# Second layer of a fused four-layer kernel: later lower parts, and four routed blocks made ahead

## The reference

```python
gates = sigmoid(x @ w_gate)                       # per token, head and expert
gm = one_hot(argmax(gates)) * gates
values = einsum('bhne,ehdk,bnd->bhnk', gm, value_experts, x)
attn = softmax(causal(q * SCALE @ k.T))
out = einsum('bhij,bhjk->bhik', attn, values)
out = einsum('bhne,ehkd,bhnk->bhnd', gm, output_experts, out).sum(axis=1)
```

## Time and profile before

| | us |
|---|---|
| median of 3 runs | 3399.88 (3398.44 to 3403.79) |
| the profiled execution | 3397.21 |
| its span | 3395.2 |
| TensorE busy in it | 3192.8 |
| granted clock, mean | 0.974 |

### The profile page before, as it was taken

The page is one execution under the profiler, slowest core; times in us unless marked ns, Lnnn a source line. Parts: engine busy times, 40 slices in busy tenths (PEclk is TensorE's granted clock), DMA queues, the critical chain, the costliest instruction groups (busy, mean ns, idle before and its releaser), DMA issues. The chain is left out here.

```text
span 3395.2 us, 49636 instructions
## 1 busy us (share of the span) xinstructions
PE 3192.8 (94%) x18098; PEld 2292.6 (68%) x18098; DVE 1852.0 (55%) x3126; ACT 1479.7 (44%) x2732; POOL 959.2 (28%) x883
## 2 busy tenths in 40 slices
PE   7998999999999999999999898999989899999998
PEld 4667656975588755986569545555455588888886
DVE  4557745675466743866455665756657423333332
ACT  3331254423543144422543575555746544444443
POOL 1213323742266512753237301103020011111110
PEclk9998999999999999999999899999999899999999
DMA  6112111011111111111111101010000210000000
GB/s 199 65 41 67 32 31 55 26 50 38 26 55 50 40 27 33 56 44 35 28 55 38 27 2 51 2 27 1 2 26 2 95 57 13 13 13 13 7 7 13
DMA packets 182672, 124.06 MB, mean 37 GB/s; under 512 B 125216, under 2 KB 163360, under 8 KB 178976
## 3 DMA queue, kind: packets, MB, share of 16 engines
q1 hardware_dynamic: 182432, 120.87, 12.7%
HBM read 103.37 MB, written 28.44 MB: 39 GB/s over the span
## 5 line engine op out<-in xcount | busy, mean ns | idle before, releaser
L1667 ACT ACTIVATE l3b_prob<-sums 128x512 f32<-128x512 f32 (+3 forms) x768 | 333.0, 494 | 169.1 <-PE sums L1578 130.9
L1939 PE MATMUL sums<-l_uhi,l_h 128*128 128x512 f32 x1024 | 405.6, 396 | 0.0
L1939 PE MATMUL sums<-l_ulo,l_h 128*128 128x512 f32 x1024 | 405.1, 396 | 0.0
L644 POOL TENSOR_TENSOR l_qrow<-l_vm,l_qst 128x512 fp32r<-128x512 f32 x256 | 352.5, 1389 | 162.0 <-ACT l_qst L638 134.5
L1027 DVE TENSOR_REDUCE l2b_mx<-sums 128x1 fp32r<-128x1024 f32 (+7 forms) x256 | 192.6, 758 | 267.2 <-PE sums L939 265.5
L964 PE MATMUL sums<-sb_nx,l_vx 128*128 128x512 f32 (+3 forms) x768 | 306.2, 509 | 2.2 <-ACT l_od L1002 2.2
L995 ACT ACTIVATE sb_nx<-sums 128x512 f32<-128x512 f32 (+3 forms) x384 | 183.4, 493 | 260.7 <-PE sums L956 255.5
L2024 DVE TENSOR_TENSOR l_ulo<-l_made,l_uhi 128x512 fp32r<-128x512 f32 x128 | 90.3, 705 | 363.4 <-ACT l_uhi L1956 363.3
L1573 PE MATMUL sums<-l_qst,l_kst 64*128 64x512 f32 (+3 forms) x768 | 276.5, 422 | 11.9 <-ACT l3b_prob L1667 5.4
L631 DVE TENSOR_TENSOR l_vm<-l_oT,sums 128x512 f32<-128x512 f32 x256 | 174.3, 683 | 166.0 <-PE sums L623 164.3
L638 ACT CAST l_qst<-l_vm 128x512 fp32r<-128x512 f32 x256 | 157.9, 620 | 243.9 <-DVE l_vm L631 231.8
(11 more groups left out here) (272 smaller groups left out, 8005.0 us busy)
## 6 DMA issues: line engine op xcount, KB each, us to landing
l_ve<-ve SPq DMA_DIRECT2D x32, 512.0 KB, 4.1
l_oe<-oe SPq DMA_DIRECT2D x16, 1024.0 KB, 5.2
between<-sb_x SPq DMA_DIRECT2D x48, 256.0 KB, 2.1
l_vm<-weights_copy SPq DMA_DIRECT2D x32, 352.0 KB, 3.4
sb_nx<-between SPq DMA_DIRECT2D x9, 1024.0 KB, 5.7
weights_copy<-h SPq DMA_DIRECT2D x2, 4096.0 KB, 26.1
l_ve<-inverse SPq DMA_DIRECT2D x32, 256.0 KB, 3.6
l_qst<-l3b_peak SPq DMA_DIRECT2D x512, 0.5 KB, 2.0
```

The lines of the kernel that those rows point to most:

```text
L644: pool.tensor_tensor(rlo[:, i % RT, :], routed[:, i % RT, :], rhi[:, i % RT, :].bitcast(F32), ALU.subtract).then_inc(s3.routed_lo, 1)
L1667: act.activation(prob[:, i % RB, j, a, 0:hi - lo], bank(m.ps, part % SCORE, 0, hi - lo), ACT.Exp, scale=SCALE1).then_inc(s.exp_ready, 1)
L1939: run(lambda out, a, x, first, last: pe.matmul(out, a, x, start=first, stop=last))
```

## The change

`lo_parts` of a projection's fourth piece moves on VectorE from tick 23 (39, 55) to tick 24 (40, 56), behind that tick's reduction. Four blocks instead of three are made ahead; their masks begin at tick 75 instead of 78, routes at 76 instead of 79, upper parts at 77 instead of 80. Block 3's mask reuses bank 4 and waits for the first route, block 4's takes bank 7 and block 5's bank 6; so the last check of the weights, which must be through with its buffer, is taken at tick 75 instead of 78. The copy of the last head's output moves from the end of ScalarE's list in attention to the start of its list in the output stage, with a semaphore `last_od` for which SP's transfer of head 7's denominators and the mask of block 5 wait. Each sequence does this.

```diff
--- before.py
+++ after.py
@@ -482,7 +482,7 @@
            "gates_hi hilo_ready gates_turned gmT_ready")
 ATTN2 = ("qk_mm qk_hi qk_parts max_mm max_read row_ready even_carried odd_carried score_mm exp_ready pv_mm o_read "
          "den_in den_turned row_in rden_in o_ready oe_in even_weight_in odd_weight_in weight_chain weight_unlike weight_taken")
-OUT2 = ("ve_in oe_in1 oe_in2 oe_in3 oe_hi oe_lo "
+OUT2 = ("last_od ve_in oe_in1 oe_in2 oe_in3 oe_hi oe_lo "
         "mask_mm routed routed_hi routed_lo out_mm y_ready last_den_in last_den_turned last_row_in last_rden_in last_o_ready")
 CLAMP = 80.0
 
@@ -528,8 +528,8 @@
     gates_hi = od[:, 1, 0:N].bitcast(F32R)
     hilo = od[:, 0, :].rearrange("p (t a n) -> p t a n", t=NT, a=2)
     blocks = [(c, e, n) for c in range(H0 // 2) for e in range(NE) for n in range(NH)]
-    MASKS, AHEAD = 3, 3
-    mask_bank = lambda i: (4, 7, 3)[i] if i < AHEAD else 4 + i % MASKS
+    MASKS, AHEAD = 3, 4
+    mask_bank = lambda i: (4, 7, 3, 4, 7)[i] if i <= AHEAD else 4 + i % MASKS
     EH = NE // 2
     half = lambda odd: slice(DH0 * odd, DH0 * odd + DH0)
     vcol = lambda h: half(h % 2)
@@ -866,8 +866,9 @@
         DIVIDED = H0 - 2
         divided_in = lambda x: divmod(x - 3 * NT, NT)
         ROW_OUT, TURNED, ROW_BACK, SPREAD, CHUNK_AT = 3, 5, 5, 7, 1
+        LAST_CHECK = 75
         SPLIT_HI, SPLIT_LO = {60: 0, 62: 1}, {73: 0, 74: 1}
-        MASK_AT, ROUTE_AT, ROUTE_HI_AT = {78: 0, 79: 1, 80: 2}, {79: 0, 80: 1, 81: 2}, {80: 0, 81: 1, 82: 2}
+        MASK_AT, ROUTE_AT, ROUTE_HI_AT = ({at + i: i for i in range(AHEAD)} for at in (75, 76, 77))
 
         def project_in(x):
             c, ahead = divmod(x - PROJECT_FROM, 2 * NT)
@@ -981,6 +982,8 @@
                         weighted(h2, k2)
                     if x in MASK_AT:
                         pe.wait_ge(s.max_read, NT * H0)
+                        if MASK_AT[x] >= MASKS:
+                            pe.wait_ge(s3.routed, MASK_AT[x] - MASKS + 1)
                         mask(pe, MASK_AT[x])
 
             @block.scalar
@@ -1015,7 +1018,6 @@
                         act.copy(ohi0[:, es, :], oe[:, es, :]).then_inc(s3.oe_hi, 1)
                     if x in ROUTE_HI_AT:
                         route_hi(act, ROUTE_HI_AT[x])
-                head_out(H0 - 1)
 
             @block.vector
             def _(dve):
@@ -1025,10 +1027,12 @@
                         t = NT - 1 - k1
                         dve.wait_ge(s.max_mm, NT * h1 + k1 + 1)
                         dve.reduce_max(mx[:, h1, t:t + 1], bank(m.ps, max_bank(h1, k1), 0, (t + 1) * P), AX_X).then_inc(s.max_read, 1)
-                    if project_in(x):
+                    if project_in(x) and project_in(x)[1] < 3:
                         lo_parts(dve, *project_in(x))
-                    if k1 == NT - 2 and h1 >= 1:
-                        dve.wait_ge(s.weight_unlike, h1)
+                    if project_in(x - 1) and project_in(x - 1)[1] == 3:
+                        lo_parts(dve, *project_in(x - 1))
+                    if (k1 == NT - 2 and 1 <= h1 < H0) or x == LAST_CHECK:
+                        dve.wait_ge(s.weight_unlike, min(h1, CHECKS))
                         dve.scalar_tensor_tensor(worst[:, :], unlike, 0.0, worst[:, :], ALU.not_equal, ALU.max).then_inc(s.weight_taken, 1)
                     over, k = divided_in(x)
                     if 0 <= over < DIVIDED and k == TURNED:
@@ -1088,7 +1092,7 @@
         stats_at = {4: 0, 5: 1, 6: 2, 7: 3}
         LAST_TURNED, last_o_at = 4, {23: (6, 0), 26: (6, 1), 29: (7, 0), 32: (7, 1)}
         VALUE_HI_AT, value_lo_at = 51, {53: 0, 55: 1}
-        PER_C = NE * NH
+        PER_C, PV = NE * NH, 5
         following = b + 1 < SEQS
         if not following:
             turn_at, x_hi_at, x_lo_at, value_lo_at, LOGITS_AT, GATES_FROM, EXP_AT, VALUE_HI_AT = {}, {}, {}, {}, None, len(blocks), None, None
@@ -1101,6 +1105,8 @@
             @block.sync
             def _(sp):
                 for h in (6, 7):
+                    if h == H0 - 1:
+                        sp.wait_ge(s.last_od, 1)
                     sp.dma_start(denp[:, h % 2, :], den_row(h)).then_inc(s.last_den_in, 16)
                 fetch_load(sp, m, sf, src[b + 1])
                 sp.wait_ge(s.oe_lo, 2)
@@ -1139,6 +1145,7 @@
                         act.wait_ge(s.out_mm, PER_C * (c - 1))
                     act.copy(ohi_of(c, es), oe[:, es, :]).then_inc(s.oe_hi, 1)
 
+                act.copy(od[:, (H0 - 1) % 2, :], m.ps[:, PV * HALF:(PV + 2) * HALF]).then_inc(s.last_od, 1)
                 for i in range(AHEAD, len(blocks)):
                     if i in split_at:
                         expert_hi(*split_at[i])
@@ -1214,6 +1221,8 @@
                 for i in range(AHEAD, len(blocks) + AHEAD):
                     if i < len(blocks):
                         pe.wait_ge(s.routed, i - MASKS + 1)
+                        if i == AHEAD + 1:
+                            pe.wait_ge(s.last_od, 1)
                         mask(pe, i)
                     k = i - AHEAD
                     c, e, n = blocks[k]
```

## The result

The changed kernel takes 3351.5 us (median of four runs, 3349.9 to 3355.8) against 3400.0 for the kernel before (four runs, 3398.4 to 3403.8): 48.5 us less. The ratio is 0.9858, with a 95% interval of 0.9846 to 0.987. Measured again beside later experiments, the same kernel had 0.9874 (0.9859 to 0.9889), 43.5 us less. The forecast was 3354, or 46 less.

What follows compares the result with a forecast made beforehand. TensorE, busy 94% of the span, was taken as the bound, with time only in idle gaps and half clock. Terms 17.0 + 15.0 + 6.0 + 6.5 + 1.5 = 46.0 us gave a 3354 us median, own bounds 3342 to 3366, rivals 3338 to 3372.

Steps and rivals of the forecast that it cites:

- The late reduction: Where heads 2, 4 and 6 begin: reducing before the lower parts wins 1.42 us 12 times, 17.0 us.
- The second gap: At the next row of maxima after each projection: TensorE waits 0.37 to 0.43 us for the delayed 896-column reduction.
- The clock: Behind the 12 projection gaps: ten half-clock stretches of TensorE go, 1.5 us each, 15.0 us.
- The border: Between attention and output experts: barrier opens 1.96 us earlier, token load 0.5 later, 1.5 us four times, 6.0 us.
- Slack in the output stage: Masks issued four blocks ahead remove waits of 0.57 and 1.60 us: 6.5 us, plus 1.5 us of halved clock.
- my slower rival: In the output stage TensorE stands before block k until route k+1; at 0.3 us per block, 3425 us; chance 0.03.

Runs made afterwards that it cites:

- The filled gaps: Kernel before with nine unused 512-column matmuls in each of the twelve 2.23 us gaps: 3378.9 us, ratio 0.9938.
- the tokens first: Changed kernel with the load of the next tokens issued ahead of both denominator transfers in the output stage: 3350.8 us, ratio 0.986.
- the lower parts alone: Kernel before with only a projection's fourth lower parts one tick later, still three blocks ahead: 3364.5 us, ratio 0.9902.
- four ahead alone: Changed kernel with a projection's fourth lower parts put back to their old tick: 3389.4 us, ratio 0.9965.

## Why the prediction was right

*The late reduction.* Forecast: a first gap of 0.38 and a second of 0.43, so 1.42 us twelve times, 17.0. In the profile the reduction stands 1.86 us earlier after the same steps and the interval behind it is 0.38 us longer than the full-clock ones of before, 1.48 each, 17.8. The second gap was the least certain size; the distance between two rows of maxima shows 0.24 of it, the interval 0.38.

*The clock.* Forecast 15.0 from ten stretches at 1.5. All ten are gone, and the 34.0 us of the heads leave 16.2 for them; the intervals behind the ten are 1.53 us longer than the two full-clock ones of before, which makes 15.3. The filled gaps, which change only this, give 15.2 in the same intervals. Cause and size are shown.

*The border.* Forecast: barrier 1.96 us earlier, gap 1.0, token load 0.5 later, wait of 1.9 before block 4, hence 1.5 us per sequence. Measured: a start 1.7 to 1.9 us earlier behind head 7's first reduction, a gap of 1.02, GpSimd done at 0.67 behind TensorE instead of 2.83, the load 0.37 later, a wait of 1.67. Up to mask 16, with one block's 1.67 us taken off for its earlier place, the four sequences have 1.4, 2.1, 1.4 and 1.4 us, 6.3 against 6.0. That the earlier start is cut down by VectorE's chain, and that halved clock there is worth nothing, is shown by the tokens first and, for the clock, by the two borders of the kernel with the lower parts alone. One reason I gave was wrong: I counted the copy out of attention as a help. It is neutral.

*Slack in the output stage.* This is the term that was mis-sized: 6.5 us and 1.5 for a halved stretch, 8.0 together; the profile gives 4.0 there, and 0.9 more at the end. The step that failed: "so a long VectorE step can be 1.67 us longer". It can for the lower part, which is what I reckoned with, but block k's matmuls also stand behind the mask of block k+4, which needs route k+1, and with three mask banks that wait did not move. It became the binding one: the waits of 0.57 and 1.60 us for GpSimd turned into several of a few tenths and one of 0.65 for VectorE. What the wait of 0.57 gave at first was taken back a few masks later (reckoned as above, the first sequence is 1.3 us ahead at mask 24, 1.9 at mask 26 and 1.4 at mask 30), and of the 1.60 us 0.85 came back in each of three sequences; the halved stretch of the third made the rest. This is the place of my slower rival, at a price of 1.2 us for masks 44 to 50 (11.2, and 10.0 in the last sequence, which has no such step) in each of three sequences instead of 0.2 per block. The earlier waits behind long steps likewise stand in front of masks now:

```profile
571.79 0.50 PE L623 MATMUL sums<-l_gmT,l_sel 128*128 128x512 f32 x1 [1.01 <-DVE l_vm L631]
...
579.61 0.50 PE L623 MATMUL sums<-l_gmT,l_sel 128*128 128x512 f32 x1 [0.47 <-DVE l_vm L631]
```

The errors of the terms (0.8, 1.2 and 0.3 too low, 3.1 too high) leave 45.2 us in the profiles of layer 2 against a forecast of 46.0. That the sum is so near is luck in part: a term of 8 us was 3 too high, and the others made up for most of it. The totals, 48.5 and 43.5, lie on both sides.

## What to carry to other kernels

When one engine serves two others, put the operation with the nearer due time first in its list: here a reduction that TensorE waited for stood behind lower parts that nobody needed for ten ticks. A short idle gap on TensorE can cost more than its own length (here 1.5 us on top of 2.23), since the clock behind it may be halved; look at the granted clock in the stretch behind each gap, and try dummy matmuls in the gap to see what it is worth. Before counting a deeper lead as slack, list every wait that the lead passes (here the ring of mask banks beside the ring of routed blocks): the shortest one decides.

## What the runs showed of the hardware

Idle time of 2.23 us between dense matmuls was followed by 3.4 us at half clock in ten of twelve cases in the profile of before and in eleven of twelve with four ahead alone, 0.36 us in none of 36 in three profiles (the changed kernel twice, the lower parts alone), and the same 2.23 us filled with matmuls in none of twelve. A gap of 3.17 us was not always followed by it either: four of four in the profile of before, one of four with the lower parts alone. And dummy matmuls, nine in each gap, which left 0.09 to 0.14 us of it idle, made a kernel 20 us faster, with VectorE's and ScalarE's work unchanged. A halved stretch where another engine set the pace cost nothing (153.76 us without, 153.80 with it).
